# A graph kernel on one Trainium2 core: five dense units move into the list phase, and the node table grows by eight units

## What is computed

```python
def _spmm(edge_src, edge_dst, edge_weight, feats, n_nodes):
    msgs = edge_weight[:, None] * feats[edge_src]
    return jax.ops.segment_sum(msgs, edge_dst, num_segments=n_nodes)
feats = [x]; cur = x                      # x: 100000 x 256, f32
for _ in range(3):
    cur = _spmm(src, dst, edge_weight, cur, 100000)      # 25000 edges, sorted by dst
    feats.append(cur)
y = concatenate(feats, axis=1) @ shared_weight + output_bias   # weight 1024 x 256
out = layernorm(x + y, eps=1e-5)
```

## Time and profile before

| | |
|---|---|
| median of 3 runs | 1518.73 us (1518.3 to 1522.41) |
| the profiled execution | 1520.6 us, of which its span is 1518.9 us |
| busy share | PE 91%, DVE 77%, POOL 71%, ACT 65% |
| granted TensorE clock, mean | 0.975 |
| DMA | 421.54 MB, mean 278 GB/s |

### The profile page before, as it was taken

How to read it: one execution, slowest core, us unless ns; L and a number is a source line. 1 busy time by engine, 2 the same in 40 slices (tenths; PEclk the granted TensorE clock), 3 DMA queues, 4 the chain that set the end, 5 groups by cost and what they waited for, 6 DMA issues and landing times. The chain is left out here.

```text
span 1518.9 us, 29487 instructions
## 1 busy us (share of the span) xinstructions
PE 1383.6 (91%) x7840; PEld 1177.3 (78%) x7840; DVE 1175.3 (77%) x4189; ACT 980.5 (65%) x2620; POOL 1076.4 (71%) x1038
## 2 busy tenths in 40 slices
PE   6999999999999986659997999999999988888887
PEld 5888888888888874448885887887877777777765
DVE  8877777777777755887875576645999999999987
ACT  4777777777777752226775555554677776777667
POOL 4577777777777787565774677776377777777774
PEclk9999999999999998989998999999999999999999
DMA  7879998999888877338986688677999999999997
GB/s 256 261 257 311 301 306 285 302 311 302 293 273 282 281 196 179 127 90 296 329 315 236 169 241 239 193 207 186 321 345 353 340 347 330 336 343 340 350 412 261
DMA packets 218638, 421.54 MB, mean 278 GB/s; under 512 B 31863, under 2 KB 136874, under 8 KB 218474
## 3 DMA queue, kind: packets, MB, share of 16 engines
q1 hardware_dynamic: 167558, 323.81, 61.4%
q0 software_dynamic: 49920, 95.13, 22.5%
q10 hardware_dynamic: 996, 0.72, 0.2%
HBM read 230.99 MB, written 201.73 MB: 285 GB/s over the span
## 5 line engine op out<-in xcount | busy, mean ns | idle before, releaser
L1493 PE MATMUL ps_y<-w_sb,xT 128*128 128x256 f32 (+1 forms) x1832 | 478.0, 390 | 18.8 <-DVE y_ring L1826 17.2
L1493 PEld LDWEIGHTS ps_y<-w_sb,xT 128*128 128x128 f32 (+1 forms) x1832 | 338.2, 196 | 60.1 <-issue 13.7
L1216 ACT ACTIVATE o_ring<-y_ring,rstd 128x256 f32<-128x256 f32 (+1 forms) x782 | 349.6, 497 | 0.0
L1832 DVE BATCH_NORM_STATS2 stats<-y_ring 128x6 f32<-128x256 f32 (+1 forms) x782 | 291.2, 414 | 4.5
L1826 DVE TENSOR_TENSOR y_ring<-ps_y,bias 128x512 f32<-128x512 f32 x290 | 199.7, 689 | 119.1 <-PE ps_y L1493 105.7
L936 POOL DMA_INDIRECT rows_in<-in_x,gather_idx x200 | 201.8, 1009 | 86.7 <-issue 66.6
L936 POOL DMA_INDIRECT tails_found<-tail_keys,table_idx x200 | 202.4, 1012 | 72.0 <-issue 58.9
L936 POOL DMA_INDIRECT rows_in<-out_rows,early_node x184 | 191.2, 1039 | 80.7 <-issue 47.0
L1578 PE MATMUL ps_u<-w_sb,cT 128*128 128x256 f32 x788 | 209.2, 388 | 7.9 <-DVE u_out L2083 7.9
L940 POOL DMA_INDIRECT out_rows<-u_out,early_node x160 | 165.4, 1034 | 54.0 <-issue 42.9
L1493 PE MATMUL ps_sum<-w_sb,xT 128*128 128x256 f32 x624 | 163.6, 388 | 26.8 <-ACT xT L1203 26.8
(11 more groups left out here) (342 smaller groups left out, 2505.6 us busy)
## 6 DMA issues: line engine op xcount, KB each, us to landing
x_ring<-in_x SPq DMA_DIRECT2D x195, 512.0 KB, 6.5
out_rows<-o_ring SPq DMA_DIRECT2D x195, 512.0 KB, 4.6
c_rows<-sums SPq DMA_DIRECT2D x49, 512.0 KB
u_rows<-u_out SPq DMA_DIRECT2D x49, 512.0 KB
keys_bc<-u_rows SPq DMA_DIRECT2D x20, 512.0 KB, 8.4
u_rows<-bias SPq DMA_DIRECT2D x15, 512.0 KB
listed<-u_rows SPq DMA_DIRECT2D x13, 512.0 KB
c_list_rows<-sums SPq DMA_DIRECT2D x11, 512.0 KB
```

The lines of the kernel that those rows point to most:

```text
L1216: last = act.activation(o_ring[slot][0:rows, r * D:(r + 1) * D], y_ring[k][0:rows, r * D:(r + 1) * D], ACT.Copy, scale=rstd[k][0:rows, r:r ...
L1493: last = pe.matmul(y_bank[p][0:rows, r * D:(r + 1) * D], columns_in[p][:, q * P:q * P + rows], w_sb[:, c, :], start=c == 0, stop=c == KC - 1)
L1832: last = dve.bn_stats(stats[k][0:rows, r, :], y_ring[k][0:rows, r * D:(r + 1) * D])
```

## The change

The five list steps that have list work get two dense units each where they had one. The other work of these steps stays as it was, the passes on DVE among it. All units behind them have a number five higher in the same place, and D has five fewer: it has 19 kept steps of 4 units (d = 3 to 21) and a last step of 3 where there were 20 kept steps of 4 and a last step of 4. The kept tiles end at 175 instead of 183. The node table begins at unit 172 instead of 180: 23 whole units and the tail, where there were 15. `fill_tab` runs for two units in a step, `add_to_tab` for tiles 171 to 196 (26, were 18), `load_tab` for 24 (were 16). Two small splits of the table of deviations (`SPLITS`, four DVE operations each) go. `tab_filled` now shares a semaphore with the weights' load.

```diff
-    B_UNIT = LIST_UNIT + ONE * LIST_ALL + STEP
+    L_SIZES = (ONE,) * LIST0 + (PAIR,) * LIST_STEPS + (ONE,)
+    B_UNIT = LIST_UNIT + sum(L_SIZES) + STEP
...
-    D_STEPS = REAL // Q
-    KEPT_STEPS = D_STEPS - 1
+    KEPT_STEPS = 22
+    D_STEPS = KEPT_STEPS + 1
...
-    D_SIZES = (0,) * E_STEPS + (FOUR,) * (D_STEPS - E_STEPS)
+    D_SIZES = (0,) * E_STEPS + (FOUR,) * (KEPT_STEPS - E_STEPS) + (STEP,)
...
-    TAB_UNIT = D_OFFS[KEPT_STEPS - 2] - STEP
+    TAB_UNIT = 172
...
-    EVEN_STEPS = KEPT_STEPS - 2
+    EVEN_STEPS = KEPT_STEPS - 1
...
-    SPLITS = ((0, 0, 82, 0), (9, 82, 130, 0), (15, 130, 154, 0), (18, 154, 168, 0), (19, 168, MAIN_END, 0),
-              (20, AGAIN, kept_window(EVEN_STEPS)[1], AGAIN), (21, kept_window(EVEN_STEPS)[1], TAB_UNIT, AGAIN))
+    SPLITS = ((0, 0, 82, 0), (9, 82, 130, 0), (15, 130, 154, 0), (18, 154, MAIN_END, 0), (20, AGAIN, TAB_UNIT, AGAIN))
...
-        tab_filled = sem("tab_filled")
+        tab_filled = weights_loaded
...
         def list_step(l):
-            return LIST_UNIT + ONE * l, ONE, 0, PAIR
+            return LIST_UNIT + sum(L_SIZES[:l]), L_SIZES[l], 0, PAIR
...
-                if a >= 2 and TAB_UNIT + a - 2 <= UNITS:
-                    fill_tab(TAB_UNIT + a - 2)
+                    sp.wait_ge(weights_loaded, 16)
+                if a >= 2:
+                    for u in range(TAB_UNIT + 2 * a - 4, min(TAB_UNIT + 2 * a - 2, UNITS + 1)):
+                        fill_tab(u)
...
-                for k in range(FOUR):
+                for k in range(dense[1]):
```

More of the change, by code:

```diff
@@ L974, in step_a @@
                 if a == TAB_TILE // Q + 1:
-                    pool.wait_ge(tab_filled, 16 * (UNITS - TAB_UNIT + 2))
+                    pool.wait_ge(tab_filled, 16 + 16 * (UNITS - TAB_UNIT + 2))
                     limit(SLOTS)
@@ L1191, in _ @@
                        PAIR: {0: 0, 2: 1, 4: 2, 6: 3}, 1: {0: 0, 4: 1}}
+            TURNED_AT = {FOUR: {q: q for q in range(Q)}, STEP: {1: 0, 2: 1, 3: 2, 5: 3, 6: 4, 7: 5}}
             ROOTS_AT = {FOUR: {1: -1, 3: 0, 5: 1, 7: 2}, STEP: {2: -1, 4: 0, 7: 1}, PAIR: {2: -1, 6: 0}, 1: {4: -1}}
@@ L1233, in dense_slot @@
                         copy_xT(LAST_PAIR)
-                    for p in turns_at.get(2 * off + q, ()):
+                    done = TURNED_AT[units].get(q)
+                    for p in turns_at.get(2 * off + done, ()) if done is not None else ():
                         copy_xT(p)
```

## The result

The changed kernel takes **1532.43 us** (median of 4, 1531.57 to 1534.6), the kernel before took 1519.03 beside it (1518.3 to 1522.41). The ratio is 1.0094, with a 95% interval from 1.0077 to 1.0111: slower by 13.4 us of the medians, where 8.4 were forecast (1527, range 1514 to 1540).

The account below looks back on a forecast made before the run. The prediction took PE to bound most of A, POOL its end, DVE the list, and DVE with transfers close behind most of D. Terms 15.0 + 16.0 - 22.6 = 8.4 us more gave 1527 us, range 1514 to 1540 (the forecast's own 1521 to 1534).

Parts of the forecast that it names:

- The adds: End of A: eight more adds on POOL delay the last look-ups, matches and list by 15.0 us; bounds 0 and 20.
- The two rivals in which little or half of this arrives: End of A: the adds' 15 us fall away (1512 us, chance 0.12), or half arrives (1520 us, chance 0.13).
- The list: Five list steps: five more units at 3.2 us of DVE each cost 16.0 us; bounds 14 and 18.
- D: Phase D: 415.1 us instead of 437.7, so 22.6 less; bounds 30 less and 15 less.
- The table steps: D's steps 17 to 20, with table loads and kept tiles: 22.85 us each, 91.4 in all; bounds 21.0 and 24.7 each.
- The lower ceiling: Rival, D's table steps: transfers fall to 343 GB/s when full for long, 17 us more, 1544 us; chance 0.03.
- Costed at nothing: Eight more table fills under PE in A, two splits removed, early gathers, B and C: taken as no cost.
- dearer table steps: Rival, D's table steps: a node-part stall in each, 24.7 us each, 7.4 more in all, 1534 us; chance 0.12.

Follow-up runs that it names:

- table_only: Changed kernel with one unit in each list step as before, larger node table kept, last two steps of D dense with four units: 1536.28 us, ratio 1.0111.
- no_early_adds: Changed kernel without the eight new adds of tiles 171 to 178 to the node table (output incomplete): 1517.0 us, ratio 0.9995.
- units_only: Kernel before, node table and kept tiles unchanged, five units moved to the list steps, last five steps of D with three units each: 1528.44 us, ratio 1.0060.
- sixteen_gathers: Kernel before with sixteen further small POOL gathers, one in each of sixteen kept steps, into a tile nothing reads: 1538.57 us, measured once.
- no_early_loads: Changed kernel taking the bias instead of table rows for units 172 to 179, leaving out 4.2 MB of loads in D (output incomplete): 1529.95 us, ratio 1.0085.
- front_old_table: Kernel before with its node table, five units moved into list steps 1 to 5: 1523.15 us, ratio 1.0032.
- free_three: Kernel before with its table, three further units in list steps 1 to 3, taken from two groups of C and D's last step: 1517.91 us, ratio 1.0001.
- list_front: Changed kernel with its two-unit steps at list steps 1 to 5 instead of 4 to 8: 1526.94 us, ratio 1.0053.
- own_semaphore: Changed kernel with a semaphore of its own for the table's fills, as before the change: 1532.67 us, ratio 1.0093.
- wide_front: Changed kernel with three units in the last two steps of A, two in list steps 1 to 3, one in 4 to 8: 1520.54 us, ratio 1.0024.
- wider_front: Changed kernel with three units in the last three steps of A and two in list steps 1 and 2: 1522.79 us, ratio 1.0026.
- after_eight: Changed kernel with eight further small POOL gathers, one in each of D's first eight kept steps: 1539.58 us, measured once.

## Why the forecast was right, and where it was not

**The adds: right.** Forecast 15.0 us. The two POOL steps took 30.8 and 36.7 us for 31 and 36 forecast, the last look-up was late by 17.0 - 1.9 = 15.1 us, and 13.8 of it was still there in list step 3. table_only shows 15.3 us with the adds and without the units, and no_early_adds is 14.4 to 15.4 faster with the units and without the adds. The two rivals in which little or half of this arrives are out. PE's clock did fall to 0.85 in the step with eight adds, which I had feared would make it 20, and no more than the 15 was lost.

**The list: right.** Forecast 16.0, measured 16.1, with DVE busy 63.01 of 66.2 us; 14.8 in units_only. A unit in a step with list work costs 3.0 to 3.2 us, about its work on DVE.

**D: the number right, its reason only in part.** Forecast 415.1 us, measured 415.0 (291.5, 91.4, 20.1 and 12.0 for 292.1, 91.4, 19.1 and 12.5). But I had read "DVE is first and the transfers close behind" from DVE's 284.56 of 292.1 us, and overlooked POOL, whose busy share there is 73%. Its timeline in the changed kernel shows the two ends of a stretch:

```profile
1119.37 0.99 POOL L938 DMA_INDIRECT rows_in<-out_rows,early_node  x1 [1.96 <-DVE sums L2694]
1121.94 0.99 POOL L938 DMA_INDIRECT rows_in<-out_rows,early_node  x1 [1.58 <-DVE sums L2694]
...
1494.27 0.97 POOL L942 DMA_INDIRECT out_rows<-u_out,early_node  x1 [0.36 <-issue]
1497.79 0.97 POOL L942 DMA_INDIRECT out_rows<-u_out,early_node  x1 [2.54 <-ACT u_out L1425]
```

From the end of the second to the end of the third there is no gap of POOL over 0.6 us in 372 us. POOL does 277 transfers in it, 1.34 us each with the gap behind, so the 16 of a kept step want 21.5 us, and the plain steps of the changed kernel take 20.8. POOL falls behind by a few transfers, and does 69 in the four table steps where 64 are due. So the kept steps are paced by POOL, with DVE, at 97%, and the transfers just behind. units_only (four units less in kept steps give 2.8 us) and sixteen_gathers (a gather more costs 1.2 us where POOL is full) show it. The forecast of this term held by luck as far as its reason goes: it held because the change takes out a whole kept step, with everything in it: had it taken five units out of D and left the kept tiles, my reading would have said about 20 us less, and 7.4 was measured.

**The table steps: right in size, each stall smaller but more of them, the bytes not alone.** Their 91.4 us are what I took, at 407 GB/s, for 9.26 x 4 = 37.04 MB (37.16 by the trace). DVE waited for node parts three times:

```profile
DVE fixed_parts L2504 <- DMA src_f<-node_parts: 5.8, 2, 3.3
DVE fixed_parts L2504 <- DMA next_f<-node_parts: 2.5, 1, 2.5
```

That is 8.3 us in the four steps, on each of which I had put half a stall of 3.9, 7.8 in all. The lower ceiling did not come: 407 GB/s held for 91 us. By the Trainium skill, DMA: Bandwidth & Descriptors, section "Where 436 GB/s comes from", these steps would have been bound at 358; the trace disagrees with it over 91 us as it did over 50. What no_early_loads adds is that only 3.2 of the 10.3 us that its 4.2 MB are worth came back. POOL, without a gap in these steps in both kernels, is the likely reason.

**Costed at nothing.** The fills show no cost (the shift stays at 1.8 to 1.9 us from step 1 of A to step 22), nor does the shared semaphore. The 1.9 us are there before anything of the change acts; the other kernels have 0.2 to 5.1 us there, without an order that I can see, and I count it as how executions differ. B, C and their bridges gave back 2.9 us, which I had not forecast and did not trace. sixteen_gathers, whose order is that of before up to D but for one gather at its end, gives back 2.3 us over the same stretch, so most of the 2.9 may be how executions differ.

**What was missing from the sum** is the end. The terms sum to 8.4 and measure 13.8 + 16.1 - 22.7 = 7.2; with -2.9 and +1.9 the work ends 6.3 us later. The rest of the span's 11.2 is POOL's closing drain, 4.9 us, of which neither a term nor a rival spoke; it is most of the distance from 8.4 to 13.4, beside the 2.2 us by which the profiled executions lie otherwise to their medians. That the result still lies in the range of 1521 to 1534 is luck as far as these 4.9 us go: the upper part of the range was there for dearer table steps, which did not come.

**What stays open** is the cause of that drain. It lasted 2.8 us in before, units_only, front_old_table and free_three, 8.8 in table_only, list_front, no_early_adds, own_semaphore, no_early_loads, wide_front, wider_front and the changed kernel, 8.2 in after_eight and 7.0 in sixteen_gathers. The shared semaphore, the new adds, the new loads and the units' place are each excluded by one of these, and so is the count of indirect transfers (1012 go with 2.8 and with 8.2 us, 996 in no_early_adds with 8.8). The larger table and the kept step fewer come together in every kernel with 8.2 or 8.8 us and are not told apart; sixteen_gathers has neither and still 7.0. What is left may be something in what POOL's program issues in D, but no run isolates it. A kernel with the front of wide_front and a drain of 2.8 us would end some 2 us ahead of before, an estimate from the medians (1520.54 - 4.9 against 1517.51); no such kernel was run.

## What to carry to other kernels

An engine that issues indirect transfers can be full at a busy share of 77% (287 of POOL's 372 us here): count its instructions times busy time plus the constant gap, and look for the longest gap, before you call another engine the bound. Work moved from a long phase to a short one is paid where it lands by what paces that place, and given back only if the thing that paces the old place moves too; here four units alone were worth 2.8 us in the kept steps of D, and a whole kept step lasts 20.8. And look at what stands behind the last computation in the records: a closing drain can take the gain of the work ahead of it.

## What the hardware showed that was not expected

- An indirect gather or scatter of 128 rows keeps POOL for 1.01 to 1.04 us in the mean of the common kinds (single ones 0.97 to 1.47), and 1.00 us with rows of 36 bytes too; one with an add takes 1.58. At least 0.3 us lie behind each. Of a gather more in a full stretch 1.2 us reached the end of the stretch.
- 407 GB/s were held for 91 us on one core, with loads, stores and POOL's gathers and scatters mixed.
- POOL's closing drain took 2.8, 7.0, 8.2 or 8.8 us, to 0.01 us the same in kernels of one kind, and its cause is open.
